# The last batch's output projection in fp16 passes, spread over the last two pairs of heads

## The reference, cut to what matters

```python
xn = _layernorm(x)
q, kv = split(xn @ Wq), split(xn @ Wkv)          # 16 heads of 16; values are the rotated keys
q, kv = _apply_rotary(freqs, q) * SCALE, _apply_rotary(freqs, kv)
attn = softmax(einsum('bmd,bnd->bmn', q, kv))
out = einsum('bij,bjd->bid', attn, kv)            # back to (b, n, 256)
x + (out @ Wout + bout) + (silu(xn @ wg.T) * (xn @ wu.T)) @ wd.T
```

## Time and profile before

| quantity | value |
|---|---|
| median of 3 runs | 831.03 us |
| the profiled execution | 833.87 us, span 832.0 us |
| TensorE busy, granted clock | 96% of the span, 0.994 |
| VectorE, ScalarE, GpSimd busy | 89%, 83%, 32% |
| loop: one pair of heads | 18.9 us |
| slot 6 of pair 30 starts; pair 31 starts | 782.77; 793.98 us |
| last values start; last matmuls (L892) start; span ends | 818.29; 825.04; 832.0 us |

### The profile page before, as it was taken

One profiled execution on the slowest core, in us unless ns is written; L12 is line 12 of the kernel. 1 busy time (PEld: TensorE's weight loads), 2 busy tenths in 40 slices (PEclk: granted clock), 3 DMA queues, 4 the chain that ended last, 5 costly groups with the idle time before them and its releaser, 6 DMA issues.

```text
span 832.0 us, 19132 instructions
## 1 busy us (share of the span) xinstructions
PE 798.9 (96%) x7316; PEld 296.3 (36%) x7316; DVE 736.4 (89%) x891; ACT 691.5 (83%) x1270; POOL 267.5 (32%) x504
## 2 busy tenths in 40 slices
PE   4988999999999999999999999999999999999997
PEld 2344555445333333333333333333333333333234
DVE  5877888888899999999999999999999999999702
ACT  4655555545799999999999999999999999999982
POOL 3785778887120001101222222222222222222210
PEclk9998999999999999999999999999999999999999
DMA  9456455554111111111221122221222212221222
GB/s 312 120 117 147 108 124 128 127 127 104 33 32 37 29 37 30 31 30 45 56 58 50 49 53 58 54 51 49 55 54 58 53 49 51 56 58 50 81 74 75
DMA packets 111680, 60.55 MB, mean 73 GB/s; under 512 B 71372, under 2 KB 101900, under 8 KB 111588
## 3 DMA queue, kind: packets, MB, share of 16 engines
q1 hardware_dynamic: 111588, 59.32, 28.2%
HBM read 28.57 MB, written 16.90 MB: 55 GB/s over the span
## 4 chain that ended last, share of the span: by engine, by line
PE 91%; ACT 3%; POOL 2%; DMA 1%; DVE 1%; issue 1%; SPq 0%; DVEq 0%; ACTq 0%; POOLq 0%
PE ps L759 34%; PE ps L776 19%; PE ps L741 15%; PE ps L636 9%; PE ps L650 4%; ACT arena L1021 2%; PE ps L613 1%; PE ps L614 1%; PE ps L615 1%; PE ps L609 1%; POOL arena L1340 1%; PE ps L685 1%; DMA x_all<-x_dram 1%; PE ps L787 1%; PE ps L803 1%
## 5 line engine op out<-in xcount | busy, mean ns | idle before, releaser
L1176 DVE TENSOR_REDUCE negmax<-ps 128x2 f32<-128x1024 f32 x512 | 588.8, 1212 | 6.5 <-PE ps L776 6.4
L1021 ACT ACTIVATE arena<-ps 128x512 f32<-128x512 f32 x1024 | 555.4, 595 | 31.7 <-PE ps L741 9.9
L759 PE MATMUL ps<-arena 128*32 128x256 f32 x4072 | 326.5, 392 | 2.4 <-issue 2.2
L741 PE MATMUL ps<-qs,ks 51*128 51x512 f16 x1024 | 197.9, 382 | 3.3 <-ACT arena L1021 2.1
L776 PE MATMUL ps<-ks,qs 48*128 48x512 f16 x972 | 189.4, 386 | 0.0
L759 PEld LDWEIGHTS ps<-arena 128*32 128x32 f32 x4072 | 80.6, 108 | 127.9 <-issue 126.8
L776 PEld LDWEIGHTS ps<-ks,qs 48*128 48x128 f16 x972 | 46.6, 92 | 195.0 <-DVE negmax L1176 140.1
L636 PE MATMUL ps<-arena,side 128*128 128x512 f16 x384 | 89.7, 382 | 4.3 <-DVE side L1121 4.3
L1444 POOL TENSOR_TENSOR arena<-arena,x_all 128x256 f32<-128x256 f32 x22 | 16.0, 728 | 232.0 <-ACT arena L1042 232.0
L741 PEld LDWEIGHTS ps<-qs,ks 51*128 51x128 f16 x1024 | 50.7, 93 | 77.8 <-ACT arena L1021 45.9
L1374 POOL TENSOR_TENSOR mparts<-rowmax,munit 128x16 f16<-128x16 f32 x32 | 7.1, 222 | 210.4 <-DVE rowmax L1186 210.4
(11 more groups left out here) (117 smaller groups left out, 516.7 us busy)
## 6 DMA issues: line engine op xcount, KB each, us to landing
parts_d<-arena SPq DMA_DIRECT2D x64, 128.0 KB
x_all<-x_dram SPq DMA_DIRECT2D x8, 512.0 KB, 9.0
qs<-parts_d SPq DMA_DIRECT2D x64, 64.0 KB, 1.9
ks<-parts_d SPq DMA_DIRECT2D x64, 64.0 KB, 1.9
o_d<-arena SPq DMA_DIRECT2D x124, 32.0 KB
arena<-o_d SPq DMA_DIRECT2D x24, 128.0 KB
arena<-inv_d SPq DMA_DIRECT2D x48, 64.0 KB
out_dram<-arena SPq DMA_DIRECT2D x24, 128.0 KB, 1.8
```

The lines of the kernel that those rows point to most:

```text
L741: mm = pe.matmul(ps[:, score_bank(place(p, kt, 2 * half + a)), :], ks[ring][top:top + ROWS, kt * P:(kt + 1) * P], qs[ring][top:top + ROWS, ...
L759: mm = pe.matmul(ps[32 * j:32 * j + 32, 7, cols], vstage[pl % 2][:, j % 2, kt, :], probs[PER_STEP * (kt % PBUF) + j][:, cols], start=(kt = ...
L1021: act.activation(probs[PER_STEP * (kt % PBUF) + j], ps[:, score_bank(place(p, kt, j)), :], ACT.Exp).then_inc(exp_done, 1)
L1176: dve.tensor_reduce(negmax[pl % 2][:, h, :, kt], ps[:, bank:bank + 2, :], AX.X, ALU.max, negate=True).then_inc(max_done, 1)
```

## The change

The fp32 projections at the end become fp16 passes of hi and lo parts, three per matmul, with the weights' scale put back when the residual is added. The last two pairs now have this order: tile 21 is late in pair 30 (slots 12 to 14), tile 22 takes slot 3 of pair 31, tile 23 is late in its slots 6 to 9. Both late tiles use bank 3. The front half's 24 passes lie one to three in a slot from slot 6 of pair 30 to slot 13 of pair 31. The front's inputs are loaded at the end of SyncE's slot 28 and divided and split on GpSimd. The sums of a pair have a semaphore of their own, `sums_in`. Tile 23 is loaded ahead of the store of pair 30's output. The store of tile 21 follows the loads of the back half. The last eight matmuls alternate between row halves, and the residual is added two tiles at a time.

```diff
+LATE_TILES = (PAIRS - LAG - 1, PAIRS - LAG + 1)
+LATE_BANK = 3
+LATE_AT = {(PAIRS - 2, 12): (0, range(0, 2)), (PAIRS - 2, 13): (0, range(2, 4)), (PAIRS - 2, 14): (0, range(4, 6)),
+           (PAIRS - 1, 6): (1, range(0, 1)), (PAIRS - 1, 7): (1, range(1, 3)), (PAIRS - 1, 8): (1, range(3, 4)),
+           (PAIRS - 1, 9): (1, range(4, 6))}
+FRONT_AT = {(PAIRS - 2, 6): range(0, 1), (PAIRS - 2, 7): range(1, 3), (PAIRS - 2, 8): range(3, 4),
+            (PAIRS - 2, 9): range(4, 6), (PAIRS - 2, 10): range(6, 7), (PAIRS - 2, 11): range(7, 9),
+            (PAIRS - 2, 15): range(9, 11), (PAIRS - 1, 0): range(11, 12), (PAIRS - 1, 1): range(12, 14),
+            (PAIRS - 1, 2): range(14, 15), (PAIRS - 1, 5): range(15, 18), (PAIRS - 1, 11): range(18, 20),
+            (PAIRS - 1, 12): range(20, 22), (PAIRS - 1, 13): range(22, 24)}
+LAST_ORDER = [t for n in range(CT) for t in (n, n + CT)]
+PAIR_ORDER = [0, 2, 1, 3]
...
# SyncE, end of slot(p)
+                if p == PAIRS - RING:
+                    for k in range(2):
+                        sp.wait_ge(inv_stored[k], 16 * QH * (p // 2))
+                    load_last_o(0, front_in)
+                    load_last_inv(0, front_in)
...
# SyncE, after slot(PAIRS - 2)
+            sp.wait_ge(divided, CREDIT + LOOP_TILES - 1)
+            load_tile(*tile_of(LOOP_TILES)[0:2], LOOP_TILES % 2)
             p = PAIRS - 1
-            sp.wait_ge(divided, CREDIT + p - LAG)
-            load_tile(*tile_of(p - LAG + 1)[0:2], (p - LAG + 1) % 2)
+            sp.wait_ge(divided, CREDIT + LOOP_TILES)
+            load_tile(*tile_of(LOOP_TILES + 1)[0:2], (LOOP_TILES + 1) % 2)
             store_o(p - 1, p - 1)
-            sp.wait_ge(divided, CREDIT + p - LAG + 1)
-            load_tile(*tile_of(p - LAG + 2)[0:2], (p - LAG + 2) % 2)
             store_inv(p - 1, p - 1)
-            store_res(*tile_of(p - LAG))
+            for k in range(2):
+                sp.wait_ge(o_stored[k], 16 * PER_STEP * (PAIRS // 2 - k))
+            load_last_o(1, back_in)
             for k in range(2):
                 sp.wait_ge(inv_stored[k], 16 * QH * (PAIRS // 2 - k))
-            load_last(1, back_in)
-            for n in range(LOOP_TILES, (BATCH - 1) * BT):
-                store_res(*tile_of(n))
+            load_last_inv(1, back_in)
+            store_res(*tile_of(LATE_TILES[0]))
+            store_res(*tile_of(tile_in_pair(p)))
+            store_res(*tile_of(LATE_TILES[1]))
...
# TensorE
+            def last_pass(t, g, rows, i):
+                tok = slice(t % CT * P, (t % CT + 1) * P)
+                pe.matmul(last_out(t), osplit[t // CT][0:rows, g, i // 2, tok], (wo_lo if i == 1 else wo_hi)[0:rows, g, :],
+                          start=(g + i + t % 2 == 0), stop=False)
...
+                    if (p, slot) == min(FRONT_AT):
+                        pe.wait_ge(max_done, MAXES * PAIRS)
+                        pe.wait_ge(front_split, 2 * CPB)
+                    if (p, slot) in LATE_AT:
+                        i, passes = LATE_AT[p, slot]
+                        n = LATE_TILES[i]
+                        tile_passes(n, n % 2, LATE_BANK, passes)
+                    for u in FRONT_AT.get((p, slot), ()):
+                        if u == 3 * 2 * LATE_BANK:
+                            pe.wait_ge(late_done, len(LATE_TILES))
+                        last_pass(u // 3, 0, P, u % 3)
...
# ScalarE, copy_o
-                    act.wait_ge(o_stored[slot % 2], 16 * (PER_STEP + 1) * (turn * (RING // 2) + slot // 2))
+                    act.wait_ge(o_stored[slot % 2], 16 * PER_STEP * (turn * (RING // 2) + slot // 2))
+                    act.wait_ge(sums_in[slot % 2], 16 * (turn * (RING // 2) + slot // 2))
...
# VectorE
+            def add_late(n):
+                dve.wait_ge(wout_done, CREDIT + n + 1)
+                dve.wait_ge(res_free[n % 2], 16 * (n // 2))
+                dve.scalar_tensor_tensor(res[n % 2], ps[:, LATE_BANK, 0:DIM], wo_unit[:, 0:1], x_all[:, n, :],
+                                         ALU.mult, ALU.add).then_inc(late_done, 1)
...
-            divide_last(0, front_in, front_divided)
+            add_late(LATE_TILES[0])
             invert(PAIRS - 2, RING - 2)
-            for n in range(LOOP_TILES, (BATCH - 1) * BT):
-                add_late(n)
-            divide_last(1, back_in, back_divided)
+            add_late(LATE_TILES[1])
+            divide_back()
...
# GpSimd
-            for j in range(FIRST_SLOT, RING):
-                n = LAST - LAG + j - FIRST_SLOT
-                slot(TURNS, j, [(n, n % 2)])
-            for n in range(LOOP_TILES, (BATCH - 1) * BT):
+            n = LAST - LAG
+            divide(n, n % 2)
+            divide_front()
+            add_tile(n, n % 2, n)
+            split_max(PAIRS - 1, RING - 1)
+            pool.wait_ge(pv_done, STEPS * (PAIRS - 2))
+            stage_values(PAIRS - 1, BATCH - 1, RING - 1, PPB - 1)
+            for n in range(LAST - LAG + 1, (BATCH - 1) * BT):
                 divide(n, n % 2)
+            n = tile_in_pair(PAIRS - 1)
+            add_tile(n, n % 2, n)
```

More of the change, by code:

```diff
@@ L211, in build @@
         olast = [carve(HG * CHUNK, F32, "p (g n) -> p g n", side, g=HG) for _ in range(2)]
-        ilast = [carve(HG * CHUNK, F32, "p (g n) -> p g n", side, g=HG) for _ in range(2)]
+        ilast_room = [carve(HG * CHUNK, F32, None, side) for _ in range(2)]
+        ilast = [r.rearrange("p (g n) -> p g n", g=HG) for r in ilast_room]
+        osplit = [r.bitcast(FP16).rearrange("p (g s n) -> p g s n", g=HG, s=2) for r in ilast_room]
         rlast = carve(BT * DIM, F32, "p (t d) -> p t d", side, t=BT)
@@ L286, in build @@
         o_stored = [sem(f"o_stored{i}") for i in range(2)]
+        sums_in = [sem(f"sums_in{i}") for i in range(2)]
         inv_done = sem("inv_done")
@@ L515, in load_last, with load_last_inv @@
                     sp.dma_start(olast[k][0:rows, g, :], o_d[BATCH - 1, g, 0:rows, tok]).then_inc(landed, 16)
+            def load_last_inv(g, landed):
+                rows = P if g == 0 else BACK_ROWS
+                for k in range(CPB):
+                    tok = slice(k * CHUNK, (k + 1) * CHUNK)
                     src = inv_groups[BATCH - 1, g, 0:rows // DH, tok]
@@ L778, in maxima, with tile_passes @@
                 mm.then_inc(max_scores, 1)
[L780 to L794, removed]
+            def tile_passes(n, k, bank, passes):
+                if passes[0] == 0:
+                    pe.wait_ge(divided, CREDIT + n + 1)
+                    if n == LATE_TILES[1]:
+                        pe.wait_ge(late_done, 1)
+                    if n == 0:
+                        pe.wait_ge(wo_split, 3)
+                for i in passes:
+                    g, half = i // 3, (atile_lo if i % 3 == 2 else atile_hi)[k]
+                    mm = pe.matmul(ps[:, bank, 0:DIM], half[:, g, :], (wo_lo if i % 3 == 1 else wo_hi)[:, g, :],
+                                   start=(i == 0), stop=(i == 3 * HG - 1))
+                if i == 3 * HG - 1:
+                    mm.then_inc(wout_done, 1)
@@ L806, in project_back @@
             def project_back(t):
-                pe.matmul(last_out(t), olast[t // CT][0:BACK_ROWS, 1, t % CT * P:(t % CT + 1) * P], wo[0:BACK_ROWS, 1, :],
-                          start=False, stop=False)
+                for i in range(3):
+                    last_pass(t, 1, BACK_ROWS, i)
             def step(turn, ls, last_turn=False):
@@ L887, in _ @@
                 project_back(t)
-            pe.wait_ge(wo_scaled, 2)
+            pe.wait_ge(wo_split, 4)
             pe.wait_ge(normed, 1)
-            for t in range(BT):
+            for t in LAST_ORDER:
                 rows = slice(t // CT * HEAD_ROWS, (t // CT + 1) * HEAD_ROWS)
@@ L1244, in invert @@
             def invert(p, slot):
[L1246 removed]
+                dve.wait_ge(sums_in[slot % 2], 16 * pairs_before(p, slot))
                 if not isinstance(p, int) or p >= 2:
@@ L1299, in _ @@
             dve.tensor_tensor(onorm, osb[(PAIRS - 1) % 2], ps[:, 5, :], ALU.mult).then_inc(normed, 1)
[L1300 to L1303, removed]
+            for n, k in enumerate(PAIR_ORDER):
+                dve.wait_ge(last_done, n + 1)
+                t = (BATCH - 1) * BT + 2 * k
+                dve.scalar_tensor_tensor(rlast[:, 2 * k:2 * k + 2, :], ps[:, k, :].rearrange("p (t d) -> p t d", t=2),
+                                         wo_unit[:, 0:1], x_all[:, t:t + 2, :], ALU.mult, ALU.add).then_inc(last_res, 1)
         @block.gpsimd
@@ L1429, in divide, with divide_front @@
                 pool.tensor_tensor(atile_lo[k], atile[k], atile_hi[k], ALU.subtract).then_inc(divided, 1)
+            def divide_front():
+                pool.wait_ge(front_in, 16 * 2 * CPB)
+                for k in range(CPB):
+                    pool.tensor_tensor(olast[k][:, 0, :], olast[k][:, 0, :], ilast[k][:, 0, :], ALU.mult
+                                       ).then_inc(front_divided, 1)
+                for k in range(CPB):
```

(9 more changed lines are left out.)

78 lines of the change are left out of this document (31 added, 47 removed).

## The result

Over 20 runs each the changed kernel took 834.42 us (832.76 to 836.99) and the kernel before 832.28 us (830.75 to 834.64): a ratio of 1.0027, interval 1.0018 to 1.0036. It is 2.1 us slower, where 1.5 us faster was forecast. By the bound of half a per cent that is no change, but it is clear of the noise and of the other sign.

The account below looks back on a forecast made before the run. TensorE, busy 96%, with VectorE and ScalarE as full in the loop; ScalarE's exponentials from 784 us, TensorE again in pair 31. -0.59 to slot 15 and -0.9 in the tail make -1.5: 829.5 from median 831.03; 8-in-10 range 826.3 to 832.0.

Parts of the forecast that it names:

- the bound of half a per cent: Whole run: 4.2 us, about what a measurement can tell from no change; faster means below 826.9, slower above 835.2.
- prices of the slots: Pairs 30 and 31: k fp16 passes cost 0.11 k + 0.10 us; slots take 1.14 with one, 1.21 with two.
- the tail's 0.9: After the last values: fp16 passes replacing fp32 records in the back half save 0.9 us together.
- The length of the wait: Slot 11 of pair 31: TensorE stands 2.43 us until VectorE has added tile 23, which needs tile 21's store landed.
- The row that I read: Pair 30's four output stores, ahead of the back half's loads: they land 1.26 us after their issue ends, at 804.46.
- The rule of about 2.3 us: Tile 21's store: 2.0 us setup and completion plus bytes over a rate, about 2.3 us for 128 KB; stall nearly vanishes.
- the store that is not held (1): Tile 21's store lands in 1.8 us, not held by the load; TensorE waits 0.23 us; 827.3 us; chance 0.25.
- Passes that fit or cost more (2): Slots with passes: no switch cost before scores gives 828.5 us, a switch of 0.20 gives 830.7; chance 0.10.
- The second wait in `copy_o` (3): ScalarE's output copy pays 0.11 us in each of 30 pairs, +3.3 us, time 832.8; chance 0.08.
- The front's loads (4): Front load delays pair 31's rows, so maxima in pair 29 wait, at most about 1.5 us; 831.0 us; chance 0.05.

Follow-up runs that it names:

- the busy TensorE: The changed kernel plus 36 matmuls with unused results ahead of the wait in slot 11 of pair 31; 833.31 us, 1.0016 of the kernel before.
- plain order: Changed kernel with tile 23 added in place, plus the last eight matmuls and four stores in tile order 0 to 7; 828.83 us, 0.9959 of the kernel before.
- the store between the loads: The changed kernel with tile 21's store issued between the back half's output loads and the wait for the inverses; 828.81 us, 0.9964 of the kernel before.

## Why the prediction was wrong

| step, from start to start | forecast | measured |
|---|---|---|
| slot 6 of pair 30 | 1.70 | 1.71 |
| slots 7 to 15 of pair 30 | 10.75 | 10.80 |
| slots 0 to 3 of pair 31 | 5.14 | 5.15 |
| slot 4's start to the end of the wait | 11.71 | 13.60 |
| of which slots 4 to 10 | 8.39 | 8.54 |
| end of the wait to slot 15 | 4.06 | 5.74 |
| slot 15 to the last values | 1.57 | 1.57 |
| last values to L919 | 5.85 | 5.93 |
| L919 to the end | 6.96 | 6.79 |

Without that part line the columns add up to 47.74 and 51.29. Before, the same stretch took 49.23 (782.77 to 832.0).

The mechanism was right: slot 11 held by `res[1]`, that by tile 21's store, that by SyncE's order. The prices of the slots were right to 0.15 us and the tail's 0.9 came out as 0.82, with 0.17 more behind it. Two terms of the sum failed: 1.89 us in the chain to the end of the wait and 1.68 behind it. They are the whole distance between the forecast of -1.5 and the 2.06 found.

*The length of the wait* was forecast as 2.43 us and measured as 4.10: the chain to its end, from slot 4's start, was 1.89 too short. Of these 0.92 lie ahead of tile 21's store (issued 8.11 us after slot 4's start instead of 7.19), 0.84 in its landing (4.84 where I had taken 4.4 less 0.4), and 0.12 in the addition and its handovers (0.64 instead of 0.52).

The 0.92 come in the main from the landing of the pair's output rows. I had the back half's loads start 3.12 us after the first of the four row stores is issued. They started 4.20 us after it (798.85 to 803.05):

```profile
798.85 2.90 SPq L457 DMA_DIRECT2D o_d<-arena  x4
...
803.05 0.84 SPq L533 DMA_DIRECT2D side<-o_d  x2
```

The chain shows the slow issue of the fourth store in this place (1.46 us; the four took 2.90 instead of 1.86). It counted for little. In three of the experiments' kernels the four were issued in 1.86 us, and SyncE then waited for the rows: the loads started 4.22, 4.46 and 4.56 us after the first store's issue, as against 4.27 to 4.76 in the five with the slow issue. The place behind the whole load was reached 6.79 us after the first store's issue with the busy TensorE and 7.01 in plain order, both with the fast issue, and 7.13 in the changed kernel; the forecast had 6.21. The row that I read, 1.26 us from the end of the issue to the landing, did not hold in the changed order. The last of these stores landed 2.71 us after its own issue began, and 2.75 to 3.25 in the experiments.

In the store's landing I had lowered the one row that I had, with an argument about the queue, while the row itself was no bound: 4.84 and 5.25 were seen later. Where the bounds come from one row each, the range must go past them. The rule of about 2.3 us that the prediction set against this row is one that the Trainium skill ("DMA: Bandwidth & Descriptors", section "Anatomy of one DMA") gives for DMAs issued from GpSimd. Here SyncE issues them, and behind the whole load the trace does not agree.

*The clock* was not in the sum at all: 1.68 us. I wrote that ScalarE runs dry, and did not ask what the idle TensorE itself would lose. Keeping it busy gave back 1.59. The trace of the kernel before had the price. In its first stage TensorE waits 4.23 us for a DMA, at a granted clock of 0.50 that had fallen a little earlier, and the clock is back only in the window of 70, with TensorE busy again from 66.54. TensorE's timeline and two windows:

```profile
66.54 0.61 PE L613 MATMUL ps<-arena 128*128 128x512 f16 x1 [4.23 <-DMA arena<-arena]
...
70.35 0.56 PE L613 MATMUL ps<-arena 128*128 128x512 f16 x1
```
```profile
63.00:64.00 1.00, 0.00 (x0) 0.00 (x0) 1.00 (x5) 0.63 (x1) 0.28 (x1) 0.50 1.15 224
...
70.00:71.00 1.00, 1.00 (x5) 0.36 (x4) 0.67 (x3) 0.91 (x2) 0.00 (x0) 0.64 0.61 199
```

The nine matmuls from 66.54 to 70.35 follow one another by some 0.42 us; from 71.19 on they follow by 0.21 to 0.22. So about 1.9 us were lost behind that wait, close to the 1.68 found here. It had to be a bound of the range.

The rivals: the store that is not held (1) was wrong for the changed kernel, where the store took 4.84 us, and its 827.3 is about where the kernels without the wait lie (828.3). Passes that fit or cost more (2) were wrong in both directions: the switch costs 0.10. The second wait in `copy_o` (3) costs nothing: tile additions on GpSimd follow one another by 18.94 us (759.50 and 778.44), and by 18.93 before. The front's loads (4) delayed nothing seen: the reductions go on with no gap but the 0.3 us once a pair that they have before too.

Three things stay open: why the output rows land later than in the kernel before; why the four stores took 2.9 to 3.5 us to issue in the changed kernel and in five experiments, and 1.86 in three (with the busy TensorE, with the store between the loads, and in plain order); and why the last six steps of a store behind the load come 2.1 us and more after the first ten in the changed kernel and with the busy TensorE.

## What to carry to other kernels

When a step is moved behind others in a queue, follow who waits for its end, not only who waits for its start: a store late in the order keeps a buffer, and with two buffers the next writer pays. A third place to write (here the residual itself, in place) cost nothing that the runs show and made a change that lost 0.3% into one that wins 0.4%. The stall of 4.1 us on TensorE cost 5.6 us, since the engine came back at half clock. Before a term is put at nothing, look for the same event elsewhere in the trace: this one stood in the first stage.

The instruction at which the chain passes through a queue need not be what sets its length. Issuing the four stores faster would have won 0.1 to 0.3 of the 0.9 us, since a later command waited for their landing. And when two DMAs that are under way count on one semaphore, the sixteenth step does not say which of them has landed.

For the work that was spread one rule held. A slot in a loop without reserve has some room on each engine, and what goes beyond it is lost in full, so deal by that room (here two in even slots, one in odd).

## What the runs showed of the hardware

- TensorE's granted clock was down within the microsecond window from 0.6 to 1.6 us after its last matmul (0.80), at half from 809, and came back in the window of 815, while TensorE was busy again from 811.47. With TensorE busy through the same wait it stayed at 1.00. In the kernel before it fell in the window of 60 (0.74), when TensorE had stood for 2.21 us (57.36 to 59.57) and was busy again.
- A 128 KB store landed in 1.7 to 2.0 us alone, 2.8 behind half of a load of 0.75 MB, and 4.4 (in the kernel before), 4.84 and 5.25 behind the whole. In the changed kernel ten of its 16 steps came within 1.8 us there, the last six from 4.0 us on.
- The last of four stores of output rows (32 KB each) landed 2.7 to 3.25 us after its issue began in the changed kernel and the eight others, whether its issue took 0.42 us or 1.46 and more. In the kernel before they had landed 1.26 us after the issue's end.
- Eight fp32 matmuls on 64 rows took 2.00 us in alternating row halves and 2.96 in one half after the other.
